# Graph network layer on one core: prologue and first block in another order, bias of the own part by TensorE

## The reference

```python
def _L0_gnn_ref(node_features, senders, receivers, edge_features, W, b_W, W_e, b_We):
    h = node_features @ W + b_W
    xi, xj = jnp.split(h, 2, axis=-1)
    xji = xj[senders] + (edge_features @ W_e + b_We)
    in_degree = segment_sum(ones, receivers)
    xji = xji / (in_degree[receivers][..., None] + 1e-06)
    return xi + segment_sum(xji, receivers)

# _L1_gnn_ref: out = symmetric-normalised neighbour sum of x @ W, + b, batch norm, leaky relu
x = _layernorm(x + _L0_gnn_ref(x, src, dst, edge_attr_128, ...), axis=-1)
x = _layernorm(x + _L1_gnn_ref(x, edge_index, ...), axis=-1)
```

## Time and profile before

| | us |
|---|---|
| median of 3 runs | 1094.9 |
| lowest, highest | 1092.94, 1095.51 |
| the profiled execution's own time | 1090.87 |
| span of the profiled execution | 1089.1 |
| VectorE, busy in the span | 741.9 (68%) |
| TensorE, busy in the span | 939.4 (86%) |

### The profile page before, as it was taken

The page is one execution under the profiler, slowest core; times in us unless marked ns, Lnnn a source line. Parts: engine busy times, 40 slices in busy tenths (PEclk is TensorE's granted clock), DMA queues, the critical chain, the costliest instruction groups (busy, mean ns, idle before and its releaser), DMA issues. The chain is left out here.

```text
span 1089.1 us, 31998 instructions
## 1 busy us (share of the span) xinstructions
PE 939.4 (86%) x12854; PEld 826.4 (76%) x12854; DVE 741.9 (68%) x1852; ACT 457.0 (42%) x828; POOL 229.1 (21%) x388
## 2 busy tenths in 40 slices
PE   0478888888888888888888888899999999999955
PEld 0476777777777777777777777788988888888855
DVE  4879999999999999799999999892000000000046
ACT  1435555555555555455555555552000000000037
POOL 4313333333333333333323332210000000000000
PEclk9899999999999999999999999999999999999978
DMA  6538999899899899789998899936577787787324
GB/s 174 202 105 304 339 340 354 307 339 333 333 324 334 325 331 353 276 286 338 335 336 307 321 336 341 382 123 266 204 303 263 299 311 265 291 309 275 131 90 149
DMA packets 88673, 308.57 MB, mean 283 GB/s; under 512 B 38948, under 2 KB 55544, under 8 KB 82632
## 3 DMA queue, kind: packets, MB, share of 16 engines
q1 hardware_dynamic: 85320, 296.79, 73.8%
q0 software_dynamic: 3200, 9.68, 2.6%
HBM read 224.64 MB, written 81.79 MB: 281 GB/s over the span
## 5 line engine op out<-in xcount | busy, mean ns | idle before, releaser
L835 ACT CAST counts<-pair_ps 128x800 bf16<-128x800 f32 x391 | 316.8, 826 | 236.5 <-PE pair_ps L664 229.9
L679 PE MATMUL x_ps<-counts,xsplit 128*128 128x256 bf16 (+1 forms) x2500 | 327.4, 271 | 3.3 <-issue 3.3
L453 DVE TENSOR_TENSOR lo_oh<-counter,lo_t 128x1024 bf16<-128x1024 bf16 x391 | 272.2, 696 | 16.0 <-PE pair_ps L664 14.5
L664 PE MATMUL pair_ps<-key_oh,lo_oh 128*128 128x100 bf16 x3128 | 210.3, 209 | 75.4 <-DVE key_oh L456 47.0
L664 PEld LDWEIGHTS pair_ps<-key_oh,lo_oh 128*128 128x128 bf16 x3128 | 176.1, 98 | 111.7 <-DVE key_oh L456 84.1
L679 PEld LDWEIGHTS x_ps<-counts,xsplit 128*128 128x128 f16 x2500 | 223.9, 98 | 35.3 <-issue 13.9
L456 DVE TENSOR_TENSOR key_oh<-counter,key_t 128x800 bf16<-128x800 bf16 x391 | 226.7, 580 | 0.0
L643 DVE TENSOR_TENSOR xsplit<-pair_ps,dinv_row 128x256 f32<-128x256 f32 (+1 forms) x25 | 10.5, 419 | 243.9 <-PE pair_ps L748 243.3
L731 PE MATMUL pair_ps<-counts,zown 128*128 128x256 bf16 (+1 forms) x1300 | 140.5, 268 | 0.0
L731 PE MATMUL pair_ps<-streams,zown 128*128 128x256 bf16 x1200 | 135.4, 273 | 0.0
L731 PEld LDWEIGHTS pair_ps<-counts,zown 128*128 128x128 f16 x1300 | 123.0, 99 | 14.8
(11 more groups left out here) (146 smaller groups left out, 828.9 us busy)
## 6 DMA issues: line engine op xcount, KB each, us to landing
streams<-in_edge_attr SPq DMA_DIRECT2D x196, 640.0 KB, 11.7
counts_kept<-counts SPq DMA_DIRECT2D x23, 3200.0 KB, 12.4
streams<-counts_kept SPq DMA_DIRECT2D x12, 3200.0 KB, 12.3
counts<-counts_kept SPq DMA_DIRECT2D x11, 3200.0 KB, 12.2
dinv_row<-dinv_rows SPq DMA_DIRECT2D x25, 128.0 KB, 4.3
edst<-in_dst SPq DMA_DIRECT2D x196, 5.0 KB
counts<-in_x SPq DMA_DIRECT2D x3, 1024.0 KB, 7.0
x_rows<-x_mem SPq DMA_DIRECT2D x24, 128.0 KB, 10.0
```

What stands on the lines that cost most here:

```text
L453: dv.tensor_tensor(lo_oh[:, at % RING, :, :, :], counter[:, :, :].unsqueeze(1).to_broadcast([P, SW // 2, P, 2]), pairs(lo_t[b % 2][:, w]). ...
L664: last = nc.tensor.matmul(pair_ps[at % 2][:, half_of, col:col + KW], lo_oh[:, at % RING, w // 2, :, w % 2], key_oh[:, at % RING, w // 2, : ...
L679: last = nc.tensor.matmul(x_ps[:, k % 2, 0:n], xsplit[:, q // 2, q % 2, :], by_hi[:, q // 2, :], start=(q == 0), stop=(q == 2 * HI - 1))
L835: a.copy(out.rearrange("p h (g n) -> p h g n", g=2), pair_ps[at % 2][:, :, 0:4 * KW].rearrange("p g (n h) -> p h g n", h=HI)).then_inc(S[" ...
```

## The change

The order of the work in the prologue and in block 0 is changed, and the bias of the own part is added in another way.

- VectorE: `largest` becomes `largest(k)` for one piece of x. Pieces 0 and 1 stand ahead of `start_of(0)`, piece 2 and the maximum over all ahead of `make_keys(0)`. `scales` moves behind the first `one_hots`, its last part (`spread_scales`) behind the second, and so does the addition of the identity to `wi` (`ready_weights`). `invert_degrees(0)` moves from the prologue to slot 4, `split_low` from slots 4, 8, 12 to 5, 9, 13. `add_bias` goes away.
- TensorE: after each matmul of `own_product` a second one with one row of ones and one row of `bi` adds the bias in PSUM (50 f32 matmuls more). `own_product(m)` moves from slot m + 1 to m + 3 and stands ahead of the transposes `turn_x(m + 1)`, which move from slot m + 1 to m + 3 too. In block 0 `edges` go from slots 5 and 11 to 9 and 14, `turn_edges` from 14 to 15.
- ScalarE: `own_out(m)` copies a group from `j_ps` to `own` in slot m + 3, ahead of `x_turned(m + 1)`. `split_high` goes to slots 2, 5 and 9, `edge_rows` of block 0 from slot 12 to 15.

GpSimd's and SyncE's code is unchanged. The diff, cut to its core:

```diff
-OWN_LAG = 5
-LOW_AT = (4, 8, 12)
+OWN_AT, HIGH_AT, LOW_AT = 2, (2, 5, 9), (5, 9, 13)
...
+            def own_out(m):
+                h, n = OWN[m]
+                act.wait_ge(S["own_done"], m + 1)
+                a.copy(own[:, h:h + n, :], j_ps[:, 0:n, :]).then_inc(S["own_added"], 1)
...
+            largest(0)
+            largest(1)
             for b in range(2):
                 start_of(b)
-            dve.wait_ge(S["w_in"], 96)
-            dve.wait_ge(S["consts"], 5)
-            dv.tensor_tensor(wi[:, :], wi[:, :], ident[:, :], ALU.add).then_inc(S["weights_ready"], 1)
+            largest(2)
             make_keys(0)
-            largest()
-            scales()
-            invert_degrees(0)
...
                         one_hots(b, s)
                     if b == 0:
+                        if s == 0:
+                            scales()
+                        if s == 1:
+                            spread_scales()
+                            ready_weights()
+                        if s == 3:
+                            check_rows()
+                        if s == 4:
+                            invert_degrees(0)
                         if s in LOW_AT:
                             split_low(LOW_AT.index(s))
-                        if s >= OWN_LAG:
-                            add_bias(s - OWN_LAG)
...
                 for k in range(n):
-                    last = nc.tensor.matmul(j_ps[:, k, :], xT[m % 2][:, k, :], wi[:, :], start=True, stop=True)
+                    nc.tensor.matmul(j_ps[:, k, :], xT[m % 2][:, k, :], wi[:, :], start=True, stop=False)
+                    last = nc.tensor.matmul(j_ps[:, k, :], ones[0:1, :], bi[0:1, :], start=False, stop=True)
...
-                        if s < len(OWN):
-                            turn_x(s)
-                        if 1 <= s <= len(OWN):
-                            own_product(s - 1)
+                        if 0 <= s - OWN_AT - 1 < len(OWN):
+                            own_product(s - OWN_AT - 1)
+                        if 0 <= s - OWN_AT < len(OWN):
+                            turn_x(s - OWN_AT)
...
-                    if s == 5 and b < NB:
+                    if s == (5 if b else 9) and b < NB:
                         edges(b, 0)
-                    if s == 11 and b < NB and groups(b) > 1:
+                    if s == (11 if b else 14) and b < NB and groups(b) > 1:
                         edges(b, 1)
...
-            act.wait_ge(S["scale_ready"], 1)
-            split_high(0)
...
-                        if s < len(OWN):
-                            x_turned(s)
-                        if 1 <= s < len(X_PIECES):
-                            split_high(s)
+                        if 0 <= s - OWN_AT - 1 < len(OWN):
+                            own_out(s - OWN_AT - 1)
+                        if 0 <= s - OWN_AT < len(OWN):
+                            x_turned(s - OWN_AT)
+                        if s in HIGH_AT:
+                            act.wait_ge(S["scale_ready"], 1)
+                            split_high(HIGH_AT.index(s))
```

More of the change, by code:

```diff
@@ L474, in edge_one_hots, with largest @@
                   .then_inc(S["e_hot"], 1)
[L476 to L483, removed]
+            def largest(k):
+                a, z = X_PIECES[k]
+                dve.wait_ge(S["x_in"][k], 16 if z < NB else 32)
+                last = dv.tensor_reduce(out=rowmax[:, 2 * a:2 * z], in_=xrows[:, 2 * a:2 * z, :], axis=AX.X,
+                                        op=ALU.max, apply_absolute_value=True)
+                if z == NB:
+                    step(last)
+                    step(dv.tensor_reduce(out=pmax[:, :], in_=rowmax[:, :], axis=AX.X, op=ALU.max))
+                    dve.sem_inc(S["pmax_ready"], 1)
             def scales():
@@ L514, in split_low, with ready_weights @@
                                         op0=ALU.mult, op1=ALU.subtract).then_inc(S["x_low"], 1)
[L516 to L520, removed]
+            def ready_weights():
+                dve.wait_ge(S["w_in"], 96)
+                dve.wait_ge(S["consts"], 5)
+                dv.tensor_tensor(wi[:, :], wi[:, :], ident[:, :], ALU.add).then_inc(S["weights_ready"], 1)
             def offset(u):
@@ L772, in _ @@
             pe.wait_ge(S["consts"], 5)
-            turn_keys(0)
             pe.wait_ge(S["pmax_ready"], 1)
             nc.tensor.transpose(few_ps[0:1, 0, 0:P], pmax[:, :], ident[:, :]).then_inc(S["pmax_out"], 1)
-            pe.wait_ge(S["few_ready"], 1)
-            nc.tensor.matmul(few_ps[:, 1, 0:4], ones[0:1, :], few[0:1, :].bitcast(F32), start=True, stop=True)\
-              .then_inc(S["few_out"], 1)
-            pe.wait_ge(S["weights_ready"], 1)
+            turn_keys(0)
             for k, (a, z) in enumerate(X_PIECES):
@@ L787, in _ @@
                     if b == 0:
-                        if s < len(OWN):
-                            turn_x(s)
-                        if 1 <= s <= len(OWN):
-                            own_product(s - 1)
+                        if s == 0:
+                            pe.wait_ge(S["few_ready"], 1)
+                            nc.tensor.matmul(few_ps[:, 1, 0:4], ones[0:1, :], few[0:1, :].bitcast(F32),
+                                             start=True, stop=True).then_inc(S["few_out"], 1)
+                        if 0 <= s - OWN_AT - 1 < len(OWN):
+                            own_product(s - OWN_AT - 1)
+                        if 0 <= s - OWN_AT < len(OWN):
+                            turn_x(s - OWN_AT)
                     if s == 1 and 0 <= u < NB:
@@ L795, in _ @@
                         turn_keys(b + 1)
-                    if s == 5 and b < NB:
+                    if s == (5 if b else 9) and b < NB:
                         edges(b, 0)
-                    if s == 11 and b < NB and groups(b) > 1:
+                    if s == (11 if b else 14) and b < NB and groups(b) > 1:
                         edges(b, 1)
-                    if s == 14 and b < NB:
+                    if s == (14 if b else 15) and b < NB:
                         turn_edges(b)
@@ L926, in _ @@
                         z_out(u)
-                    if s == 12 and b < NB:
+                    if s == (12 if b else 15) and b < NB:
                         edge_rows(b)
```

7 lines of the change are left out of this document (2 added, 5 removed).

## The result

The change is slower: 1137.26 us (median of 4 runs, 1131.84 to 1140.12) against 1095.2 us (4 runs, 1092.94 to 1099.13) for the kernel before. The ratio is 1.0365, with a 95% interval of 1.0327 to 1.0404. The forecast was 1096, and its range ended at 1103.

What follows compares the result with a forecast made beforehand. VectorE's queue was taken to set the pace from block 1 on. The 8.2 us earlier start was outweighed by added wait, clock and longer trips; after block 1's give-back, +1 us remained: span 1090.1, median 1096, range 1090 to 1103.

Steps and rivals of the forecast that it cites:

- The start: Prologue, VectorE: maxima of x fill its waits, so first one-hots start at 23.85 instead of 32.08, 8.2 us earlier.
- what this gives by slot 4: VectorE's queue up to the inverse of the degrees sums to 12.6 us; `invert_degrees(0)` ends at 36.5.
- A wait that this adds: Block 0: ScalarE stands some 8 us for GpSimd's `pad_degrees(1)`, ending at 43.5; `own_product(1)` starts at 45.8 instead of 48.39.
- The clock: TensorE, after its wait: 1.4 us (0.9 to 1.9) added once for a first group starting at the lower level, 1.2 GHz.
- The round trip: Block 0, between two `own_product` through ScalarE's copies: 3.35 us instead of 2.01; eleven trips give 36.9.
- bias passes: Round-trip term for a group's one-row bias loads on TensorE: 0.97 us, bounds 0 and 1.96.
- What block 1 gives back: `count(1, 0)` to `count(2, 0)` takes 22.1 us instead of 26.95, leaving `count(2, 0)` 0.6 us later, rounded to +1.
- The other queues: `add_bias` leaving VectorE is worth nothing in block 0; SyncE's later store of counts costs nothing to 1 us more.
- the first one: Faster: `own_product(1)` near 39.5 without standing behind the degrees, 1088 (chance 0.1); or one-row passes nearly free, 1085 (chance 0.1).
- The slower one: One-row loads keep the prologue's proportion: up to 1101 at 0.147 us each with other terms, 1107 at 0.245; chance 0.32.

Runs made afterwards that it cites:

- e1_no_bias: The changed kernel with the bias matmuls of the own part left out; ratio 0.9916 to the kernel before.
- e2_full_rows: The changed kernel with the bias matmuls on 128 rows, the identity as weights and `bi` as data; ratio 0.9969 to the kernel before.
- e4_half_rows: The changed kernel with the bias matmul on 64 rows of the identity, so half of a tile's nodes get no bias; ratio 1.0318 to the kernel before.
- e3_batched: The changed kernel with a group's four products first and its four one-row biases behind them; ratio 1.0040 to the kernel before.
- e6_full_early: The changed kernel with the bias on 128 rows and `invert_degrees(0)` in slot 1 instead of 4; ratio 0.9887 to the kernel before.
- e7_early: The changed kernel, its one-row bias kept, with `invert_degrees(0)` in slot 1 instead of 4; ratio 1.0349 to the kernel before.
- e9: The changed kernel with one-row biases for two tiles at a time, behind their two products; ratio 1.0283 to the kernel before.

## Why the prediction was wrong

- *The start* and *what this gives by slot 4*: right. First one-hots 23.81 (23.85 forecast), inverse at 35.99 to 36.16 (36.5).
- *A wait that this adds*: right. ScalarE stands 9.19 us ("some 8"), GpSimd's `pad_degrees(1)` ends at 42.78 (43.5), `own_product(1)` is at 44.75 (45.8). The cast beside `split_low` was held until `split_low` ended, so the rule of the Trainium skill that I weighed there ("SBUF — State Buffer", "Who interferes with whom") holds in this run nearly whole. The cast took 2.15 us instead of 0.21 in the kernel before, a hold of 1.9 us, inside my bounds; the base of 5.7 us was 1.1 too long (6.53 from 36.25 to 42.78, less the hold), so that the two errors partly cancel.
- *The clock*: wrong, and the larger part of the loss. I added 1.4 us once, for a first group that starts at the lower level. With full-row loads that was enough: e1_no_bias and e2_full_rows were back by the second group. With loads of one and 128 rows by turns the lower level stayed for nearly all of block 0. With the eight changes in place the trip is 7.58 at the lower level and 4.66 at the higher (e4_half_rows): 2.9 us a trip.
- *The round trip*: this is the step that failed first, in the term "bias passes". I took 0.97 us for a group and gave 1.96 as the bound, because I priced one-row passes as if they were added to the product's and left those as they were. A group's eight matmuls took 5.79 us in place of 1.20 + 0.97 = 2.17. The e2_full_rows trip of 3.22, and 0.90 of it for the bias against e1_no_bias, says that 0.97 was the right size for a pass of the same rows. What I missed is that two kinds of load alternate, which also changes the price of the four products (e4_half_rows and e3_batched). At the higher level that is 4.66 - 3.22 = 1.4 us a trip, some 16 us in eleven; against the 3.35 that I had summed it is 1.3 a trip, 14 us, and by this estimate the median would have come to 1110, past my range, with the clock as forecast.
- Together 2.9 + 1.4 = 4.4 us a trip (7.58 against 3.22), 48 us in eleven, less for the groups at the higher level. The split hangs on the order: taken at the lower level, the changes cost 2.3 (7.58 against 5.30) and the level 2.1. Both have one cause, as the level stays down only in the versions whose loads change rows (e6_full_early against e7_early). Measured from `own_product(1)` to `own_product(12)`: 87.97 us, forecast 42.3; e2_full_rows took 41.6.
- *What block 1 gives back*: right in kind. `count(1, 0)` to `count(2, 0)` took 23.4 us instead of 26.95; the forecast was 22.1.
- *The other queues*: the late store went out at 146.54, and the delay at `count(2, 0)` leaves it and all the rest no more than the 2 us between 46.9 and 49.1.
- *The rivals*: the first one priced `own_product(1)` without standing behind the degrees at 7.7 us; e6_full_early, with full rows, shows 8.9 at `own_product(12)`, so the order of the inverse was a loss that I had seen and priced about right. The slower one had the right place and sign, but its price ended at 0.245 a load, 1107. The rule of the Trainium skill that I quoted ("TensorE: Matmul & The Clock Gate", "Why this matters for your kernels": fewer rows take the same time) is borne out by e3_batched, where one-row loads in a row cost what full ones cost; where they alternate with full ones both kinds still take the same time, but both take more, which the rule by itself doesn't foresee.

Shown: that the change of rows between loads is what costs (e2, e3, e4 and e9), that the lower level stays with such changes and not without them, where nothing but the operands of the bias matmul differs (e6 against e7), and that the rest of the change is a gain (e1, and e6 with the earlier inverse; e2 by 0.3% only). Open: why the level stays down; why the higher one comes back behind an edge group, for one to three groups, and in e3_batched already in the fourth group; and why a load after a change of rows waits. The 0.22 us gap fits a load that isn't laid over the matmul ahead of it, since the spacing 0.72 is its 0.50 of loading plus the gap, but no run separates the two.

## What to carry to other kernels

Before a small matmul is put between others, compare the rows that its weights fill with those of its neighbours (1, 64 and 128 were run here). Give it the same rows, here the identity and a full tile in place of one row of ones; that gave a ratio of 0.9969. Putting all of its kind in a row, which gave 1.0040, is second best. When a term is to be bounded by the nearest row, ask whether that row stood alone or between other kinds; a price taken from a group of equal loads (x8) isn't one for loads in turn. And price a step by what it does to its neighbours too, times the number of trips of the loop that it stands in.

## What the hardware showed that I had not expected

- A load whose rows differ from those of the load ahead (1 or 64 against 128, either way) begins behind an idle 0.22 us at the lower level. An f32 matmul then takes 0.72 us instead of 0.43, and 0.42 instead of 0.22 at the higher level.
- TensorE stayed at the lower level's durations while the profile, which models the ends of matmuls, has it busy for 29.95 us or more of 30, in the change, e4_half_rows, e7_early and e9_pairs. The weight loads covered 21.56 (e4_half_rows, 60 to 90 us) to 24.39 us (e9_pairs, 50 to 80).
- The granted clock of a stretch read 1.00 and later 0.50 with the same durations (0.72 per matmul, 0.86 for eight `count` loads), so it alone doesn't tell the level.
